# Second layer of a fused attention kernel: eight buffer sets, and the memory products as a step of their own

## What is computed

```python
memory_proj = einsum('bme,de->bmd', memory, W_mem)            # W_mem 256 x 128
scores = einsum('bnd,bmd->bnm', hidden, memory_proj) / sqrt(256)
attn = softmax(scores)
memory_context = einsum('bnm,bmd->bnd', attn, memory_proj)
gate = sigmoid(concat([hidden, memory_context]) @ W_gate + b_gate)   # W_gate 512 x 256
fused = hidden + gate * memory_context
out = fused * rsqrt(mean(fused**2) + 1e-6) * norm_w
```

## Time and profile before

| | us |
|---|---|
| three runs | 522.04, 522.23, 524.18 (median 522.23) |
| profiled execution | 521.07 |
| its span, first to last instruction | 518.9 |
| mean granted TensorE clock | 0.963 of 2.4 GHz |
| PE busy | 435.7 (84% of the span) |
| DVE busy | 353.8 (68%) |
| ACT busy | 257.0 (50%) |
| POOL busy | 152.0 (29%) |

### The profile page before, as it was taken

How to read it: one execution, slowest core, us unless ns; L and a number is a source line. 1 busy time by engine, 2 the same in 40 slices (tenths; PEclk the granted TensorE clock), 3 DMA queues, 4 the chain that set the end, 5 groups by cost and what they waited for, 6 DMA issues and landing times.

```text
span 518.9 us, 10981 instructions
## 1 busy us (share of the span) xinstructions
PE 435.7 (84%) x3842; PEld 337.3 (65%) x3842; DVE 353.8 (68%) x804; ACT 257.0 (50%) x726; POOL 152.0 (29%) x268
## 2 busy tenths in 40 slices
PE   1098669997899999999999999999997986898992
PEld 1076538675577777776776776776866875676771
DVE  5934468797698698698699599699682650535543
ACT  0356456663554564464464564464451432655662
POOL 3585233113123123113114114013012103446542
PEclk9999958999999999999999999999997997999996
DMA  7587763633103103103103103001004001112111
GB/s 244 187 283 237 250 243 129 197 126 123 32 20 95 42 11 104 42 1 113 42 1 113 42 3 113 25 18 52 9 4 142 22 20 51 32 51 69 54 42 41
DMA packets 29492, 44.44 MB, mean 86 GB/s; under 512 B 4224, under 2 KB 22528, under 8 KB 29440
## 3 DMA queue, kind: packets, MB, share of 16 engines
q1 hardware_dynamic: 25792, 31.12, 18.4%
q0 software_dynamic: 3648, 12.62, 7.4%
HBM read 27.34 MB, written 16.38 MB: 84 GB/s over the span
## 4 chain that ended last, share of the span: by engine, by line
PE 59%; DVE 18%; ACT 7%; issue 5%; DMA 5%; POOL 4%; POOLq 0%; SPq 0%; ACTq 0%; DVEq 0%
PE xyz L1444 6%; PE xyz L1485 5%; DVE E L1094 4%; PE xyz L1471 4%; PE b_ps L1598 4%; DVE mx L1092 4%; PE b_ps L1361 3%; PE b_ps L1362 3%; PE b_ps L1363 3%; POOL x_rows L1277 3%; PE xyz L1648 2%; PE xyz L1361 2%; PE xyz L1362 2%; PE xyz L1363 2%; PE xyz L1553 2%
## 5 line engine op out<-in xcount | busy, mean ns | idle before, releaser
L1092 DVE TENSOR_REDUCE mx<-xyz 128x8 f32<-128x512 f32 x64 | 43.8, 684 | 13.9 <-PE xyz L1444 13.7
L1094 DVE TENSOR_TENSOR E<-xyz,mx 128x512 f32<-128x512 f32 x64 | 44.3, 692 | 2.2
L1444 PE MATMUL xyz<-kT,qT 32*64 32x128 f32 (+1 forms) x768 | 44.3, 333 | 1.7
L1471 PE MATMUL xyz<-cst,E 128*128 128x128 f32 x256 | 37.2, 283 | 5.7 <-ACT E L787 2.8
L1598 PE MATMUL b_ps<-w_gu_hi,ms_hi 128*128 (+2 forms) x90 | 38.0, 422 | 3.9 <-ACT ms_hi L811 3.9
L1314 POOL TENSOR_TENSOR mvar<-mss,pow_eps 128x1 f32<-128x1 f32 x17 | 3.2, 188 | 121.2 <-ACT m_sqr L803 119.2
L1471 PEld LDWEIGHTS xyz<-cst,E 128*128 128x128 f32 x256 | 28.7, 143 | 14.7 <-ACT E L787 6.2
L1485 PEld LDWEIGHTS xyz<-vb,kT 128*64 128x64 f32 x1024 | 32.4, 138 | 6.7 <-issue 6.5
L1485 PE MATMUL xyz<-vb,kT 128*64 128x18 f32 (+1 forms) x1024 | 35.7, 219 | 0.0
L1598 PE MATMUL b_ps<-w_gu_lo,ms_hi 128*128 (+2 forms) x90 | 34.5, 384 | 0.0
L251 POOL TENSOR_TENSOR qk<-E 128x256 f32<-128x256 f32 x16 | 13.3, 834 | 72.1 <-DVE E L1074 71.9
(11 more groups left out here) (273 smaller groups left out, 1251.5 us busy)
## 6 DMA issues: line engine op xcount, KB each, us to landing
qkv_rows<-qrow SPq DMA_DIRECT2D x18, 384.0 KB, 2.7
xq<-x_rows SPq DMA_DIRECT2D x18, 128.0 KB, 2.5
xm<-h_rows SPq DMA_DIRECT2D x17, 128.0 KB, 2.6
h_rows<-xm SPq DMA_DIRECT2D x17, 128.0 KB
x_sb<-in_x_dram SPq DMA_DIRECT2D x8, 256.0 KB, 2.8
E<-in_x_dram SPq DMA_DIRECT2D x2, 512.0 KB, 7.0
kT<-in_x_dram SPq DMA_DIRECT2D x2, 512.0 KB, 8.4
ctxT_a<-in_ctxT_dram SPq DMA_DIRECT2D x8, 128.0 KB, 2.3
```

Source lines behind the costliest of these rows:

```text
L1092: dve.tensor_reduce(mx[:, t, heads], s, AX.X, ALU.max).then_inc(max_ready, 1)
L1094: dve.tensor_tensor(E[t][:, b * 512:(b + 1) * 512].rearrange("p (h k) -> p h k", k=SEQ), s, mx[:, t, heads].unsqueeze(2).to_broadcast([P, ...
L1444: last = pe.matmul(xy[t][q, hp, o:o + w], qT[t][rows, c, q], kT[t][rows, (2 * c + b) * w:(2 * c + b + 1) * w], start=not masked, stop=True ...
L1471: last = pe.transpose(xy[t][:, a // 4, (a % 4) * P:(a % 4 + 1) * P], E[t][:, a * P:(a + 1) * P], ident)
```

## The change

In the second layer:

- Eight sets instead of four (`NB = 8`), with a PSUM bank each: the two banks `Y` and the two banks `B` join `Z` and `X`. The SBUF of sets 4 to 7 lies over the attention's buffers, which are dead by then.
- The rows (`h3`) and the results (`out_rows`) have a place of their own for all 16 tiles, over the expert weights. `h3_in` waits for `h3T_ready` of the tile four before (`N_IN = 4` semaphores), and stores hold no set.
- Both memory products become one product of 512 columns, a step of its own, `mem`, with one ACT copy out of the bank into `mpg`. For tiles 0 to 7 `mem` stands in MID: tile 0's ahead of the last `down` on PE, tiles 1 to 7 behind it. From tile 8 on it waits for `gm_ready` of the tile eight before.
- The copy of `h3T` is 256 columns. The product with `W_gate`'s upper half moves from `hw` to `gate`, where it accumulates in PSUM with the context's gate part. Its ACT copy and POOL's bias addition go; DVE adds the bias in `gate`.
- The scores are divided by their row sum before the transpose (128x128, DVE), in place of the halving of the inverted sum; the half of the sigmoid is in the scale of `mem`'s copy (0.5), and twice the fold evens it out for the gate.
- The orders of MID and L1 are written anew; the orders of the stages before are the same. In MID `load_cb` stands behind `m_out:14`.

```diff
-NB = 4
+NB = 8
+N_IN = 4
@@ buffers
+        w_gu, late_rows = [], []
+        for s in ("hi", "lo"):
+            with nc.sbuf_tensor(f"over_gu_{s}", [P, N_TILES, H], F32) as rows:
+                late_rows.append(rows)
+            w_gu.append(sb(f"w_gu_{s}", [P, 2, HC, 2 * INTER], F32R))
+        h3, out_rows = [[rows[:, i, :] for i in range(N_TILES)] for rows in late_rows]
...
-        L = [Z[0], X[0], Z[1], X[1]]
+        L = [Z[0], Z[1], X[0], X[1], Y[0], Y[1], B[0][:, :], B[1][:, :]]
@@ MID
                 sp="""
-                    m_in:13 m_in:14 m_in:15 load_cb:0 m_out:13 m_in:16 m_out:14 m_out:15 m_out:16""",
+                    m_in:13 m_in:14 m_in:15 m_out:13 m_in:16 m_out:14 load_cb:0 m_out:15 m_out:16""",
                 act="""
...
+                    hT1:16 mem:0 mem:1 mem:2 mem:3 mem:4 mem:5 mem:6 mem:7""",
                 pe="""
-                    miT:13 gu0:13 gu1:13 gu2:13 miT:14 miT:15 hT0:13 gu0:14 gu1:14 hT1:13 down:13 gu2:14 hT0:14 gu0:15
-                    gu1:15 hT1:14 down:14 miT:16 gu2:15 hT0:15 gu0:16 hT1:15 gu1:16 gu2:16 down:15 hT0:16 hT1:16
-                    down:16""",
+                    miT:13 gu0:13 gu1:13 gu2:13 miT:14 miT:15 hT0:13 gu0:14 hT1:13 gu1:14 down:13 hT0:14 gu2:14 gu0:15
+                    gu1:15 hT1:14 down:14 miT:16 gu2:15 gu0:16 hT0:15 hT1:15 gu1:16 gu2:16 down:15 hT0:16 hT1:16 mem:0
+                    down:16 mem:1 mem:2 mem:3 mem:4 mem:5 mem:6 mem:7""",
@@ L1
                 act="""
+                    h3T:0 h3T:1 hw:0 hw:1 h3T:2 h3T:3 mscore:0 hw:2 hw:3 h3T:4 attnT:0 mscore:1 mscore:2 hw:4 attnT:1
+                    gate:0 mscore:3 h3T:5 attnT:2 h3T:6 attnT:3 h3T:7 gate:1 hw:5 fuse:0 mscore:4 attnT:4 mem:8 gate:2
...
                 pool="""
+                    h3_in:0 h3_in:1 h3_in:2 h3_in:3 h3_in:4 h3_in:5 h3_in:7 h3_in:6 h3_in:9 h3_in:8 fuse:0 h3_in:11
+                    h3_in:10 fuse:1 fuse:2 h3_in:12 fuse:3 h3_in:13 fuse:4 h3_in:15 h3_in:14 fuse:5 fuse:6 fuse:7
...
                 pe="""
-                    h3T:0 h3T:1 hw:0 h3T:2 hw:1 mscore:0 hw:2 mscore:1 attnT:0 h3T:3 gate:0 mscore:2 attnT:1 hw:3
-                    gate:1 attnT:2 mscore:3 gate:2 attnT:3 gate:3 h3T:4 hw:4 h3T:5 mscore:4 hw:5 h3T:6 attnT:4
...
+                    h3T:0 h3T:1 hw:0 hw:1 mscore:0 h3T:2 mscore:1 h3T:3 hw:2 hw:3 h3T:4 mscore:2 attnT:0 mscore:3 hw:4
+                    gate:0 attnT:1 attnT:2 h3T:5 mscore:4 gate:1 h3T:6 h3T:7 attnT:3 hw:5 gate:2 mscore:5 hw:6 mem:8
+                    attnT:4 gate:3 mem:9 hw:7 mscore:6 attnT:5 gate:4 mscore:7 h3T:8 gate:5 h3T:9 attnT:6 hw:8 mem:10
...
+                    attnT:10 hw:14 h3T:15 mscore:13 attnT:11 mscore:14 attnT:12 hw:15 gate:9 mscore:15 attnT:13
+                    attnT:14 gate:10 gate:11 attnT:15 gate:12 gate:13 gate:14 gate:15""",
@@ ACT
+            def mem(n, t):
+                u, turn = late_set(n, t)
+                act.wait_ge(S["mem_ps"], tl(n, t))
+                act.activation(mpg[u], L[u], ACT.Copy, scale=0.5).then_inc(S["mem_ready"], 1)
...
-                act.activation(h3m[u], L[u], ACT.Copy).then_inc(S["h3T_ready"], 1)
+                act.activation(h3T[u], L[u][:, 0:H].rearrange("p (c q) -> p c q", c=HC), ACT.Copy).then_inc(S["h3T_ready"], 1)
...
-                if turn:
-                    act.wait_ge(stored[u], 16 * turn)
-                act.activation(z[u], L[u][:, H:2 * H], ACT.Copy).then_inc(S["g1_ready"], 1)
...
-                act.activation(mpg[u], L[u][:, H:2 * H], ACT.Copy).then_inc(S["mpg_ready"], 1)
@@ DVE
-                dve.tensor_scalar(mm[:, u, 3:4], mm[:, u, 2:3], 0.5, None, ALU.mult).then_inc(S["mrec"], 1)
+                dve.tensor_scalar(mw[u], mw[u], mm[:, u, 2:3], None, ALU.mult).then_inc(S["mrec"], 1)
...
-                dve.scalar_tensor_tensor(out=z[u], in0=L[u][:, H:2 * H], scalar=mm[:, u, 2:3], in1=z[u],
-                                         op0=ALU.mult, op1=ALU.add).then_inc(S["zb_ready"], 1)
+                dve.tensor_tensor(z[u], L[u][:, H:2 * H], b_gate[:, :], ALU.add).then_inc(S["zb_ready"], 1)
...
-                dve.scalar_tensor_tensor(out=h3[u], in0=z[u], scalar=mm[:, u, 3:4], in1=h3[u],
-                                         op0=ALU.mult, op1=ALU.add).then_inc(S["fused_ready"], 1)
+                dve.tensor_tensor(h3[i], z[u], h3[i], ALU.add).then_inc(S["fused_ready"], 1)
@@ POOL
-                if turn:
-                    pool.wait_ge(S["out_ready"], i + 1 - NB)
+                if i >= N_IN:
+                    pool.wait_ge(S["h3T_ready"], i + 1 - N_IN)
...
-            def hw(n, t):
...
-                pool.tensor_tensor(z[u], z[u], b_gate[:, :], ALU.add).then_inc(S["g1b_ready"], 1)
@@ PE
+            def mem(n, t):
+                i, (u, turn) = index(n, t), late_set(n, t)
+                if i == 0:
+                    pe.wait_ge(S["ld_cb"], 16 * 4)
+                    pe.wait_ge(S["catt_ready"], N_TILES)
+                if turn:
+                    pe.wait_ge(S["gm_ready"], i + 1 - NB)
+                elif u >= 2:
+                    pe.wait_ge(S["y_ready"], N_SLOT - 2 + u % 2 if u < 6 else N_SLOT)
+                pe.matmul(L[u], memory(n, t), w_memT[:, :], start=True, stop=True).then_inc(S["mem_ps"], 1)
...
-                pe.wait_ge(S["mexp"], tl(n, t))
-                pe.wait_ge(S["mpg_ready"], tl(n, t))
+                pe.wait_ge(S["mrec"], 2 * tl(n, t))
                 pe.transpose(L[u][:, P:2 * P], mw[u], ident).then_inc(S["mwT_ps"], 1)
...
-                pe.matmul(L[u][:, 0:H], mwT[u], mp[u], start=True, stop=True)
-                pe.matmul(L[u][:, H:2 * H], mwT[u], mpg[u], start=True, stop=True).then_inc(S["gate_ps"], 1)
+                pe.matmul(L[u][:, 0:H], mwT[u], mpg[u][:, 0:H], start=True, stop=True)
+                for c in range(HC):
+                    pe.matmul(L[u][:, H:2 * H], h3T[u][:, c, :], w_gate[:, c, :], start=(c == 0), stop=False)
+                pe.matmul(L[u][:, H:2 * H], mwT[u], mpg[u][:, H:2 * H], start=False, stop=True).then_inc(S["gate_ps"], 1)
```

More of the change, by code:

```diff
@@ L155, in xattn_kernel @@
         rstd4 = sb("rstd4", [P, NB])
+        with nc.sbuf_tensor("over_att", [P, 4, 6 * H], F32) as over_att:
+            pass
         qk = [sb(f"qk{t}", [P, 2 * H]) for t in range(TILES)]
@@ L334, in landed @@
             return sum(32 if N_DENSE + 2 * HC <= j < N_GU else 16 for j in range(k % NSTAGE, k + 1, NSTAGE))
-        stored = [sem(f"stored{u}") for u in range(NB)]
+        stored = sem("stored")
         wload = [sem(f"wload{k}") for k in range(NSTAGE)]
@@ L544, in xattn_kernel @@
                 act="""
[L545 to L549, removed]
@@ L615, in store @@
             def store(n, t):
-                i, (u, turn) = index(n, t), late_set(n, t)
+                i = index(n, t)
                 sp.wait_ge(S["out_ready"], i + 1)
-                sp.dma_start(out[i * P:(i + 1) * P, :], z[u]).then_inc(stored[u], 16)
+                sp.dma_start(out[i * P:(i + 1) * P, :], out_rows[i]).then_inc(stored, 16)
             def m_in(n, t):
@@ L689, in _ @@
                                load_cb=load_ctx_b, store=store))
-            for u in range(NB):
-                sp.wait_ge(stored[u], 16 * N_TILES // NB)
+            sp.wait_ge(stored, 16 * N_TILES)
         @block.scalar
@@ L1333, in h3_in @@
                         pool.wait_ge(S[f"st_m{k}"], 16 * ((N_SLOT + NX - 1 - k) // NX))
[L1334 to L1344 removed]
+                if i >= N_IN:
+                    pool.wait_ge(S["h3T_ready"], i + 1 - N_IN)
+                pool.indirect_dma_start(out=h3[i], out_offset=None, in_=h3_rows,
+                                        in_offset=bass.IndirectOffsetOnAxis(ap=slot_i[:, i:i + 1], axis=0)).then_inc(S[f"ld_h3{i % N_IN}"], 16)
             def fuse(n, t):
@@ L1631, in memory @@
                 return ctx_all[i // 4][:, i % 4 * P:(i % 4 + 1) * P]
+            def mem(n, t):
+                i, (u, turn) = index(n, t), late_set(n, t)
+                if i == 0:
+                    pe.wait_ge(S["ld_cb"], 16 * 4)
+                    pe.wait_ge(S["catt_ready"], N_TILES)
+                if turn:
+                    pe.wait_ge(S["gm_ready"], i + 1 - NB)
+                elif u >= 2:
+                    pe.wait_ge(S["y_ready"], N_SLOT - 2 + u % 2 if u < 6 else N_SLOT)
+                pe.matmul(L[u], memory(n, t), w_memT[:, :], start=True, stop=True).then_inc(S["mem_ps"], 1)
             def h3T_(n, t):
-                u, turn = late_set(n, t)
-                pe.wait_ge(S[f"ld_h3{u}"], 16 * turn + 16)
+                i, (u, turn) = index(n, t), late_set(n, t)
+                pe.wait_ge(S[f"ld_h3{i % N_IN}"], 16 * (i // N_IN) + 16)
+                pe.wait_ge(S["mem_ready"], tl(n, t))
                 for c in range(HC):
-                    last = pe.transpose(L[u][:, c * P:(c + 1) * P], h3[u][:, c * P:(c + 1) * P], ident)
-                if first(n) and t == 0:
-                    pe.wait_ge(S["ld_cb"], 16 * 4)
```

(7 more changed lines are left out.)

100 lines of the change are left out of this document (42 added, 58 removed).

## The result

The changed kernel takes 499.26 us (median of 4 runs, 498.08 to 501.78) against 522.13 before (median of four runs): ratio 0.956, 95% interval 0.952 to 0.961. Faster, as forecast, but by 22.9 us where 17.7 were forecast. The profiled execution took 498.49 us, its span is 496.7.

The account below looks back on a forecast made before the run. PE was taken to bound the second layer, with waits and a slow clock on top. From 433.35, 54.2 us of work, 1.7 of start gaps and 2.7 of waits save 17.7 us: 503.4 profiled, 504.5 median, range 499.5 to 511.5.

Parts of the forecast that it names:

- Where the gain lies: Second layer: PE bounds; 15.6 of its 76.7 us are waits and slow clock; 6.9 us of work leaves.
- Expert tiles: Before the layer: order changed in places, same instructions; 0 us, bounds 0.5 either way.
- Load of the memory: SP's queue, behind tile 14's store: landed at about 421.7 us, needed at 423.5, margin 1.8 us.
- Memory products in the gap: Before the layer: tiles 1 to 7 take 6.0 us from 427.3 until 433.35, hidden; slow clock's 3.0 us gained.
- Start of the layer: Until 438 us: PE gaps of 0.8 before the second tile, 0.6 before the fourth, some 0.3 more; together 1.7 us.
- Waits inside: In the layer: 2.7 us of PE waits, a quarter between bounds of 0 and 9.8 us.
- PE's work: In the layer: 61.1 us for 16 tiles less 8 x 0.86 gives 54.2 us, block mask counted at 0.19.
- ACT 34.0, DVE 33.7, POOL 23.8 us: Busy times in the layer: 33.3, near 36 and 24 us forecast, none above two thirds of the span.
- The sum: Layer from 433.35: 54.2 + 1.7 + 2.7 us, PE ends at 492.0 instead of 509.7; 17.7 us less.
- The range: Whole kernel: 499.5 to 511.5 us, taking in the forecast, rival 2, most of rival 1 and the expert tiles' 0.5 us.
- Rivals 1 and 2: Layer: waits keep their 18% share, 511.5 us, chance 0.17; clock falls once, 506.1 to 507.6 us, chance 0.12.
- Rival 4: Layer: hand-written orders serialise tiles; at 1.15 tiles on their way 529 us, slower; chance 0.03.

Follow-up runs that it names:

- e8: Changed kernel with the last expert tiles' orders as in the kernel before, memory load included: 498.37 us against 498.49.
- e12: Changed kernel with at most four tiles open and the layer's orders remade by list schedule: 509.22 us against 510.44 for the changed kernel.
- e11: e4 with the layer's orders on PE, ACT, DVE and POOL remade by list schedule: 516.54 us against 528.50 for the kernel before, ratio 0.977.
- e15: Kernel before, rows still in the ring, only the layer's orders remade by list schedule: 519.72 us against 521.09, ratio 0.997.
- e9: Changed kernel with two useless ACT copies and one useless POOL addition per tile put back: 501.98 us, ratio to before 0.961.
- e6: Changed kernel with the layer's old orders on PE, ACT and DVE: 549.16 us against 506.90 for the changed kernel, 527.68 before.
- e4: Kernel before with own buffers for rows in and out and earlier fetches, other orders kept: 521.10 us against 521.28, ratio 1.002.
- e7: Changed kernel, but fetches from tile 8 on also wait for the result of the tile eight before: 532.31 us against 506.90 for the changed kernel.
- e1: Changed kernel with the memory products of tiles 1 to 7 moved from the gap into the layer: 505.99 us against 498.49.
- e5: Changed kernel with the block mask's product done four times a tile, 48 more products: 498.54 us, ratio to before 0.959.

## Why the prediction was right and wrong

**The size was wrong.** 504.5 us was forecast and 499.26 measured, just under the low end of 499.5. The steps, one by one:

- *Where the gain lies*: right. PE bounds; the layer loses its waits, its slow clock and 6.9 us of work. At full clock 72.1 us become 60.6 by order and rows, then 54.2 by the rest; the clock is the other 4.6 of the 22.5 us, in the one profile of the kernel before.
- *Expert tiles*: 0 within 0.5 forecast; their last product ends 0.2 us later, and e8 shows no difference.
- *Load of the memory*: no wait, but the margin was smaller than I worked out. SP's queue issues it at 417.31 to 419.14 and a landing takes 4.1 us (median), so up to about 423.2, where 421.7 was forecast; the product begins at 423.69. Half a microsecond was left, not 1.8.

```profile
417.31 1.83 SPq L618 DMA_DIRECT2D over_w<-in_ctxT_dram  x4
```

- *Memory products in the gap*: until 433.3 forecast and measured, with the clock at 1.00.
- *Start of the layer*: 1.7 us of gaps forecast, 0.8 measured, ahead of the second tile. The other gaps of my walk didn't come: hw and mscore of the first two tiles fill them. On the slower kind of chip they did: PE was idle 2.3 and 1.5 us of the first 6.
- *Waits inside*: 2.7 forecast, none in the list of PE's waits. **This is the term that failed**: "I choose a quarter, because eight tiles can be open". A share of the old waits was no measure for the new ones. e12 shows that the eight tiles had no part in it, e11 and e15 that order and rows together took away all of the old waits, and with those the value was the lower bound, 0.
- *PE's work*: 54.2 us forecast. The mask's 0.19 came from one row, and that row isn't typical. In the kernel before, 11 rows of the chain have the mask straight behind another step of PE: nine show 0.06 to 0.09 us, two 0.19. (Between 461.61 and 461.72 stands the transpose L1671 of 0.11 us, no pause.)

```profile
440.78 0.06 PE xyz L1663
...
488.71 0.06 PE xyz L1663
```

With 0.06 the sum for 16 tiles falls by 16 x 0.13 = 2.1 to 52.1 us; PE was busy 53.3 to 53.4 in the three profiles with a layer of 54 us, so 1.2 us are hand-overs inside the busy time. The term was 0.9 too high.
- *ACT 34.0, DVE 33.7, POOL 23.8 us*: 33.3, 36 and 24 forecast. The normalisation takes 0.287 us, the upper bound that I took. That none of them bounds is right. That they cost nothing held for this load; e9 shows that it was no matter of their shares alone (3 us for the old load).

```profile
L1212 DVE TENSOR_SCALAR over_att<-over_att,mm 128x128 f32<-128x128 f32 x8 | 2.3, 287 | 0.3
```

- *Behind PE's end*: 9.2 us forecast and measured.
- *The sum*: 58.6 us of layer forecast (54.2 + 1.7 + 2.7), 54.2 measured: 4.4. The time outside the span was 1.8 us, not 2.2, and the median lies 0.8 over the profiled execution, not 1.2. Together that is the 5.2 us by which the forecast was high.
- *The range*: its low end came from waits of 0 and gaps of 0.5 with the work at its full 54.2, which gives 500.5, and from the 0.5 of the expert tiles, 500.0; for the 499.5 that was named the working has no term. The work had no lower bound of its own, although the 0.19 rested on one row, and the spread of single runs (498.1 to 501.8 for one kernel) wasn't in it.
- *Rivals 1 and 2* (waits keep their share, clock falls) didn't come. In the layer's first 6 us in one profile on the slower kind of chip PE was busy only 3.69 us and the clock stayed at 1.00. *Rival 4* is real and had too small a price: 529 us forecast, at 1.15 tiles on their way; e6, with little more than one tile at a time, took 1.040 times the kernel before, which is 543 us beside its 522.

**The clock, rule and row.** The kernel before shows the clock fall behind a stretch in which PE was thinly busy and its longest pause was 1.25 us. In e6 no wait of PE in the list is longer than 2.6 us, and the clock was 0.83 and 0.77 in two stretches of 10 us:

```profile
450.00:460.00 10.00, 7.25 (x27) 5.29 (x27) 3.37 (x12) 3.05 (x12) 1.75 (x3) 0.83 0.05 16
460.00:470.00 10.00, 6.16 (x17) 4.33 (x18) 3.57 (x12) 2.21 (x9) 1.48 (x4) 0.77 0.13 39
```

The Trainium skill (TensorE: Matmul & The Clock Gate, HAM oscillation) gives as its abstract rule that PE shouldn't stand idle for over some 3 us. In neither stretch was it broken, and by the rule alone the clock would have stayed up; e6's layer would then have taken some 88.8 us, an estimate from its 95.5 at a mean of 0.93. The traces say that keeping to the rule isn't enough. In the changed kernel this made no difference, since the longest pause of PE in its layer is 0.8 us, or 1.4 on the slower kind of chip, and its clock stayed at 1.00.

## What to carry to other kernels

A ring of buffers and the order of the steps are one thing. In this kernel own buffers gained next to nothing until the order used them (e4, e11), and an order that puts results late cost 24 us with the ring (e7), so cost and test them together. When all waits of a stretch hang on buffers and order, weigh the bounding engine's bare work as a likely value, and not only a share of the old waits. Read a step's cost from all its rows in the chain and not from one: here one row said 0.19 us and nine said 0.06 to 0.09. A step that puts another engine into the path of a tile (by e6's chain the normalisation on DVE) can make the old order wrong even where it takes work away.

## What the runs showed of the hardware

- Around the idle gap ahead of the layer the granted clock stayed at its lower level for 6.8 us, wherever that began. In half-microsecond slices of five kernels: before 432.3 to 439.1, e1 431.3 to 438.1, e4 433.8 to 440.6, e15 433.2 to 440.0, e11 438.1 to 444.9. It fell 5.1, 4.6, 3.2, 2.9 and 2.6 us behind PE's last product, and rose 6.1, 5.6, 4.3, 3.9 and 3.4 us after PE had begun again. The sooner it falls behind PE's last product, the more of those 6.8 us passes while PE is idle anyway: the layer's start ran at 0.52 in the kernel before and at 0.71 in e11, whose six us ahead of the layer and first six in it are below. The second fall of the kernel before was shorter, 3.2 us at 0.54, so 6.8 us is what this gap shows and no constant.

```profile
435.50:441.50 6.00, 0.25 (x3) 0.05 (x2) 0.42 (x1) 0.00 (x0) 2.23 (x3) 0.72 0.15 44
441.50:447.50 6.00, 6.00 (x28) 4.89 (x29) 0.00 (x0) 2.49 (x6) 4.28 (x5) 0.71 0.36 109
```

- A product's recorded duration says little of its price. The mask product's record is 0.22 us long, in e5 it costs 0.052 us of the layer, and the chain shows it at 0.06.
- Kernels took 1 to 2% longer on some chips than on others with the same instructions, most of it ahead of the layer (in the changed kernel it starts at 429.7 to 434.0 us on one kind, at 441.2 and 442.4 on the other), so that two experiments can be compared only by a stretch of the trace or by their ratio to a kernel that ran beside them.
